# Row statistics and the splitting of rows moved to other slots, row loads and stores to SyncE, first rows prepared in another order

## The chip, the cores and the metric

The kernel runs on one core of one Trainium2 chip. The metric is the device time of one execution in microseconds. The kernel before took 2895.55 us, the median of three runs (2894.34 to 2897.94). All times below are microseconds unless they say otherwise; time points count from the start of the profiled span.

## The reference

A state-space layer makes 128 "image" rows for each of 32 sequences, 77 text rows are put behind them, and one attention block and one linear block with a residual each follow. Cut to what matters:

```python
h = concatenate([tok(log_dt, Lambda, x, 1024), txt], axis=1)   # (32, 205, 1024)
h = h + attn(layernorm(h), wq, wk, wv, wo)                     # causal, 32 heads of 32, 8 key/value heads
h = h + ffn(layernorm(h), W_base, b_base, enc0, enc1, coefs0, coefs1, mask0, mask1)
```

```python
q, k, v = x @ wq, x @ wk, x @ wv
scores = einsum('bihd,bjhd->bhij', q, repeat(k, 4)) * SCALE    # masked causally
out = softmax(scores) @ repeat(v, 4)                            # then @ wo
```

## The kernel before

The program has three stages with a barrier between them. The first (`ssm`) makes the rows `hcat` in 16 chunks of eight channels, the second (`attention`) writes the attention output `acat`, and the third (`tail`) does the output projection, the second layer norm and the linear block over 52 tiles of rows. float32 accuracy comes from products of float16 halves: a value is parted into a high half, rounded, and a low half, the rest; each product takes three matmuls (high by high, high by low, low by high).

**Steps.** `attention` is a pipeline over sequences, one a step. `steps` runs `step(b)` on each engine for b from -4 to 32; `parts(b)` says which parts a step has. In step b the scores, the softmax and the weighing of values are those of sequence b ("att"), the row maxima those of b + 1 ("max"), the q, k and v projections those of b + 2 ("qkv"), rows b + 3 are transposed ("turn") and the layer norm is that of b + 4 ("ln"). So steps -4 to -1 fill the pipeline, steps 0 to 27 are full, and steps 28 to 32 drain it. No planner orders the work: the order on each engine is the order of the code, and semaphores tie the engines together.

**Slots.** A step has eight slots g, one for each key/value head (lines 918 to 970 on VectorE, 755 to 801 on ScalarE, 1059 to 1101 on TensorE). A slot holds the q unit g and, by the table `EXTRA` (line 493), in slots 0 to 3 a second unit: v 0, v 1, k 0, k 1. A "unit" is 24 matmuls into one of two PSUM banks `psJ`; a unit waits until the unit before the last has been read out (`pj_lo`). Slot 0 also has the unit m 1 and slot 4 the unit m 0, which transpose the row maxima.

On TensorE a slot runs: two score matmuls (`scores`, L981), score rows for the maxima (`score_rows`, L1024, L1028, L1031), the first half of the q unit, the third score matmul (L984), more score rows, the second half of the q unit, `weigh` (L1010) for the slot before, the extra unit. The third score matmul takes the PSUM bank of the first and so waits for ScalarE's first exponential of the slot (`exp_done`).

On ScalarE a slot runs: three exponentials (L783), three casts into `ph` (L790, each after GpSimd's causal mask, L699), the read-out of each unit (L796, L798; each waits for its unit), and in slots 4 to 7 `high_part` (L732 and L734), which centres and scales one quarter of the rows x and casts it to `xfh`. ScalarE also issues DMAs: in slot 2 `store(b - 1, 1)` and then the copies `values` of the transposed v (L742), in slot 3 the `load` of rows b + 5, in slot 6 `store(b, 0)`. These stand ahead of the slot's exponentials.

On VectorE a slot runs: `take_maxes` (L879, L885), the low half of the last unit (`split_unit`, L893), the subtraction for `pl` (L936), then row work, then `norm` of the head before (L833, L836) and the low halves of all but the slot's last unit. The row work is `layer_norm` in slots 1 to 3 (L852 and L853 twice, then the three operations of `rsqrt_guess`) and `low_part` (L862), which writes a quarter of `xfl`: piece 0 in slot 6, pieces 1 and 2 in slot 7, piece 3 in slot 0 of the next step. GpSimd masks, does two thirds of `pl` (L704) and, after slot 3, the Newton rounds of the inverse square root (`scale_rows`, L1135 to L1138, and `nmean`, L673).

On SP (SyncE) a step issues in this order: the restacking copies of k and q halves of the step before (`restack`, L578), `m` rows (L629, L630), the transposes of rows b + 3 (`turn`, L635 high, L636 low, for the image rows and then the text rows), the restacking of k 0 and q 0 to 3, four transposes of v (L622), `m` rows again. In step 30 the weights of the tail (`ahead`, fourteen loads, L604) stand between.

**First rows.** In steps -4 and -3 the layer norm of rows 0 and 1 runs beside the splitting of the weights: ScalarE's `weights_high` (L748) and VectorE's `weights_low` (L819), eight pieces of q weights and eight of k and v weights. TensorE's first unit waits for both transposed halves of rows 0 and for the q weights, the second for the k and v weights.

**End of the first stage.** At the last chunk SP stores the peaks of the weights to memory, waits, reads them back to all partitions (L174, L176), and only then issues the four row stores of that chunk (L180).

Of the kernel before, what the change touches and what calls it, by code (L numbers as in the profile page):

```python
# [16 lines left out]
P = 128  # L17
B = 32
# [52 lines left out]
def ssm(nc, x, txt, log_dt, lam, hcat, acat, ahead, st_k, peaks, all_peaks, peaks_in):  # L71
# [5 lines left out]
    with ExitStack() as ctx:  # L77
# [82 lines left out]
        def _(sp):  # L160
# [99 lines left out]
        def _(dve):  # L260
# [112 lines left out]
            for ch in range(NCH):  # L373
# [14 lines left out]
            dve.tensor_reduce(peaks[:, 0:1], pieces[:, 0:8], AX.X, ALU.max)  # L388
            dve.tensor_reduce(peaks[:, 1:2], pieces[:, 8:12], AX.X, ALU.max).then_inc(peaks_ok, 1)
# [32 lines left out]
def attention(nc, ahead, hcat, acat, st, qkv, arena, all_peaks, peaks_in, ksc, spare):  # L422
# [7 lines left out]
    with ExitStack() as ctx:  # L430
# [36 lines left out]
        rs = sb("rs", [P, 4, 2])  # L467
        nmean = sb("nmean", [P, 2])
# [24 lines left out]
        EXTRA = {0: ("v", 0), 1: ("v", 1), 2: ("k", 0), 3: ("k", 1)}  # L493
# [79 lines left out]
        def _(sp):  # L573
# [9 lines left out]
            def step(b, par, has):  # L583
# [15 lines left out]
                if b == B - 2:  # L599

                    for q in v_in:
                        sp.wait_ge(q, 32 * B)
                    for dst, src, arrived in ahead:
                        sp.dma_start(dst, src).then_inc(arrived, 16)  # L604
                if has["turn"]:
# [3 lines left out]
                    turn(1, nxt, b + 3)  # L609
                if has["qkv"]:  # L610
# [6 lines left out]
                    wait(sp, v_ok, 2 * (b + 2))  # L617
                    if b == -2:
                        sp.wait_ge(values_ok, 1)
                    for c in range(2):  # L620
                        for k in range(2):
                            sp.dma_start_transpose(out=vt[:, k, :, c * P:(c + 1) * P], in_=vst[k][:, c, :]).then_inc(v_in[c], 16)  # L622
                if has["max"]:

                    wait(sp, pj_lo, base + at(rows, "m", 0) + 1)
                    shift_rows(0, nxt)

# [15 lines left out]
        def _(pool):  # L643
# [855 lines left out]
```

## Time and profile before

| what | us |
|---|---|
| median of three runs | 2895.55 |
| the profiled execution's own time | 2894.3 |
| its span, first to last instruction | 2891.9 |
| TensorE busy | 2655.3 (92%) |
| VectorE busy | 1941.2 (67%) |
| ScalarE busy | 1230.0 (43%) |
| GpSimd busy | 1144.9 (40%) |
| first stage | 0 to 185.3 |
| attention stage | 185.3 to 1747.0 |
| tail | 1747.0 to 2891.9 |

Busy shares are means over stages with different limits. Matmuls are pipelined, so their listed durations overlap and a busy TensorE need not be at its peak; where two stretches hold the same matmuls, the shorter one tells what was lost in the other. In a timeline a row has the start, the duration, the engine (with q: its sequencer issues a DMA), the line, the operation, output and inputs by name, the shapes and the count; in brackets stands the idle time of the engine before it and what ended it. A busy view has a stretch and its length, then for each engine its busy time and the instructions, then the granted clock of TensorE (1.00 is 2.4 GHz, 0.50 is 1.2 GHz), the busy share of the DMA engines and GB/s.

### The profile page before, as it was taken

Reading aid. Unit: us, or ns where it says so; the run is one execution under the profiler, and the core shown is the slowest. Engines: PE = TensorE matmul, PEld = TensorE weight load, DVE = VectorE, ACT = ScalarE, POOL = GpSimd, SP = SyncE. Lnnn points to the kernel's source line nnn. Section 1 sums busy time; section 2 is a strip of 40 time slices with the busy share of each in tenths; the row PEclk is TensorE's granted clock in tenths of the full one; section 3 lists DMA queues with packets and bytes.
Section 4 is the critical chain, followed back from the end, with each engine's and each line's share of the span. In section 5 each row is a group of like instructions: output and inputs, shape, how many; then the busy total and the mean of one; then the engine's idle time right before and its main releaser. Section 6 shows DMA issues by size and latency. Waiting matters only on the chain. (4 is left out here: it accounts for less than half of the span.)

```text
span 2891.9 us, 70053 instructions
## 1 busy us (share of the span) xinstructions
PE 2655.3 (92%) x27456; PEld 1919.6 (66%) x27456; DVE 1941.2 (67%) x5569; ACT 1230.0 (43%) x2570; POOL 1144.9 (40%) x1810
## 2 busy tenths in 40 slices
PE   1948999999999999999999976999999999999999
PEld 1838888888888888888888952444444444444444
DVE  8966888888888888888888674644444444444443
ACT  4343676766767676766667572201000010101010
POOL 2751565656656565666656570101010101010100
PEclk9979999999999999999999976999999999999999
DMA  7756556465555555565555454454545455545553
GB/s 242 194 122 100 98 92 105 85 109 93 96 94 96 103 93 104 84 107 92 101 92 86 73 124 170 113 139 116 133 122 136 119 134 121 133 123 131 125 129 77
DMA packets 509031, 332.99 MB, mean 115 GB/s; under 512 B 421145, under 2 KB 464409, under 8 KB 508225
## 3 DMA queue, kind: packets, MB, share of 16 engines
q1 hardware_dynamic: 486192, 264.68, 46.3%
q10 hardware_dynamic: 22512, 63.84, 7.1%
q8 instruction: 219, 3.59, 0.6%
q14 instruction: 108, 0.88, 0.1%
HBM read 116.49 MB, written 80.61 MB: 68 GB/s over the span
## 5 line engine op out<-in xcount | busy, mean ns | idle before, releaser
L1044 PE MATMUL psJ<-xth,qh 128*128 128x205 f16 x2048 | 517.3, 253 | 51.6 <-DMA xtl<-xfl 47.6
L704 POOL TENSOR_TENSOR pl<-arena,ph 128x410 f16<-128x410 f32 (+1 forms) x512 | 501.0, 998 | 94.7 <-ACT ph L790 94.7
L1046 PE MATMUL psJ<-xth,ql 128*128 128x205 f16 x2048 | 516.3, 252 | 0.0
L1045 PE MATMUL psJ<-xtl,qh 128*128 128x205 f16 x2048 | 515.8, 252 | 0.0
L699 POOL TENSOR_SCALAR_AFFINE_SELECT arena<-arena 128x256 f32<-128x256 f32 (+1 forms) x768 | 331.7, 438 | 438.3 <-ACT arena L783 419.3
L1261 POOL TENSOR_TENSOR arena<-stage,arena 128x1024 f32<-128x1024 f32 x52 | 122.1, 2349 | 936.2 <-DVE stage L1304 936.2
L1275 ACT CAST xh<-arena 128x1024 f16<-128x1024 f32 x52 | 54.3, 1045 | 995.1 <-DVE arena L1313 995.1
L783 ACT ACTIVATE arena<-psT,escale 128x410 f32<-128x410 f32 (+1 forms) x768 | 399.6, 565 | 95.5 <-PE psT L984 57.5
L790 ACT CAST ph<-arena 128x410 f16<-128x410 f32 (+1 forms) x768 | 334.8, 500 | 14.9 <-POOL arena L699 14.7
L1304 DVE SCALAR_TENSOR_TENSOR stage<-ps5O,osc,h_in 128x512 f32<-128x512 f32 x104 | 77.9, 750 | 388.4 <-PE ps5O L1401 388.4
L885 DVE TENSOR_REDUCE mx<-psS 77x2 f32<-77x410 f32 x512 | 296.5, 579 | 60.7 <-PE psS L1031 57.0
L1399 PE MATMUL ps5F<-wfh,xth 128*128 128x512 f16 x832 | 315.4, 379 | 3.4 <-DMA xtl<-xl 2.3
L1400 PE MATMUL ps5O<-wol,ath 128*128 128x512 f16 x832 | 316.1, 380 | 0.0
L1399 PE MATMUL ps5O<-woh,ath 128*128 128x512 f16 x832 | 316.1, 380 | 0.0
L1401 PE MATMUL ps5O<-woh,atl 128*128 128x512 f16 x832 | 316.0, 380 | 0.0
L1400 PE MATMUL ps5F<-wfl,xth 128*128 128x512 f16 x832 | 315.3, 379 | 0.0
L1401 PE MATMUL ps5F<-wfh,xtl 128*128 128x512 f16 x832 | 315.3, 379 | 0.0
L879 DVE CUSTOM_DVE_ANT_0 seen<-psS,mask 128x128 bf16<-128x128 f32 x1024 | 235.4, 286 | 82.7 <-PE psS L1024 82.0
L1010 PE MATMUL psO<-vh,ph 128*128 128x33 f16 (+1 forms) x3072 | 261.0, 178 | 5.0 <-issue 4.6
L1010 PE MATMUL psO<-vl,ph 128*128 128x33 f16 (+1 forms) x3072 | 260.0, 178 | 0.0
L1010 PE MATMUL psO<-vh,pl 128*128 128x33 f16 (+1 forms) x3072 | 260.0, 178 | 0.0
L1046 PE MATMUL psJ<-xth,kl 128*128 128x205 f16 x1024 | 257.8, 252 | 0.0
(231 smaller groups left out, 6106.2 us busy)
## 6 DMA issues: line engine op xcount, KB each, us to landing
a_in<-acat SPq DMA_DIRECT2D x52, 512.0 KB, 3.8
h_in<-hcat SPq DMA_DIRECT2D x52, 512.0 KB, 4.6
qst<-qsh SPq DMA_DIRECT2D x128, 205.0 KB, 4.7
out<-stage SPq DMA_DIRECT2D x51, 512.0 KB, 3.1
hcat<-ob SPq DMA_DIRECT2D x64, 256.0 KB, 4.4
xin<-hcat ACTq DMA_DIRECT2D x32, 512.0 KB
acat<-arena ACTq DMA_DIRECT2D x64, 256.0 KB
qst<-qsl SPq DMA_DIRECT2D x64, 205.0 KB, 5.7
```

The lines of the kernel that those rows point to most:

```text
L699: pool.affine_select(out=v, in_=v, compare_op=ALU.is_ge, fill=0.0, base=0, pattern=[[0, v.shape[1]], [1, w]], channel_multiplier=-1).then_ ...
L704: pool.tensor_tensor(view(pl, g % 2, k), view(p32, g % 2, k), view(ph, g % 2, k), ALU.subtract).then_inc(lo_pool, 1)
L783: act.activation(view(p32, g % 2, k), ps_view(psT[(g + k) % 2], k), ACT.Exp, scale=(escale[:, 0:1] if k < 2 else escale[0:TXT, 0:1])).then ...
L790: act.copy(view(ph, g % 2, k), view(p32, g % 2, k)).then_inc(hi_done, 1)
L885: dve.tensor_reduce(dst, v, AX.X, ALU.max).then_inc(s_read, 1)
L1010: m = pe.matmul(o[:, t, r, :], p, v[0:T[j], j, g, :], start=n == 0, stop=n == len(list_) - 1)
L1044: pe.matmul(ps[:, 0:S], wh[:, k, c], xth[:, par, k, 0:S], start=k == 0, stop=False)
L1045: pe.matmul(ps[:, 0:S], wh[:, k, c], xtl[:, par, k, 0:S], start=False, stop=False)
L1046: m = pe.matmul(ps[:, 0:S], wl[:, k, c], xth[:, par, k, 0:S], start=False, stop=k == KC - 1)
L1399: pe.matmul(ps[h][:], th[:, k, :], wh[:, k, c], start=k == 0, stop=False)
L1400: pe.matmul(ps[h][:], th[:, k, :], wl[:, k, c], start=False, stop=False)
L1401: m = pe.matmul(ps[h][:], tl[:, k, :], wh[:, k, c], start=False, stop=k == KC - 1)
```

## The change

It changes the tables of slots. Extra units move from slots 0 to 3 to slots 1 to 4. `high_part` and `low_part` now treat rows b + 3 instead of b + 4: high pieces in slots 1, 2 and 3 (two in the last), low pieces in slots 2, 3 and 4. `layer_norm` stays in slots 1 to 3 but its place is behind `low_part`, and its first piece waits for `ln_done` of the rows before; `rs` and `nmean` get two buffers. GpSimd's `scale_rows` moves to slot 4. The two copies of `values` move into slots 1 and 2, behind the casts to `ph`. `load` and `store` are issued by SP, whose order in a step is new: v transposes come ahead of the row transposes, `turn` takes the high half as soon as it is there, and the text rows' transposes come behind the restacking. The tail's small weight loads are spread over steps 1 to 13 and the 4 MB one goes to the end of step 29. In the filling steps rows 1 are loaded only once rows 0 have landed, rows 0 get their Newton rounds on VectorE, and their low halves are put between the splits of the weights. In the first stage the reductions for the peaks start two chunks earlier and their round trip starts a chunk earlier. Left out of the diff below are renamed indices (`rs[:, b % 2]`, `nmean[:, b % 2]`, `m` for `b + 4`) and GpSimd's memsets of `ph` and `pl`, which now clear only the third block.

```diff
--- before.py
+++ after.py
...
             for ch in range(NCH):
-                if ch == NCH - 1:
+                if ch == NCH - 2:
...
+                if ch == NCH - 1:
...
-                if ch >= NCH - 12:
-                    weight_peak(ch - (NCH - 12))
-            dve.wait_ge(piece_ok, 12)
...
+                if NCH - 14 <= ch < NCH - 2:
+                    weight_peak(ch - (NCH - 14))
+                if ch == NCH - 3:
+                    dve.wait_ge(piece_ok, 12)
...
         @block.tensor
...
-        EXTRA = {0: ("v", 0), 1: ("v", 1), 2: ("k", 0), 3: ("k", 1)}
+        EXTRA = {1: ("v", 0), 2: ("v", 1), 3: ("k", 0), 4: ("k", 1)}
+        HIGH, LOW, LINK = {1: (0,), 2: (1,), 3: (2, 3)}, {2: (0,), 3: (1,), 4: (2, 3)}, {1: 0, 2: 1, 3: 2}
...
-                if b == B - 2:
-                    for q in v_in:
-                        sp.wait_ge(q, 32 * B)
-                    for dst, src, arrived in ahead:
-                        sp.dma_start(dst, src).then_inc(arrived, 16)
-                if has["turn"]:
-                    wait(sp, pj_filled, base)
-                    turn(0, nxt, b + 3)
-                    turn(1, nxt, b + 3)
+                if has["last"]:
+                    store(b - 1, 1)
                 if has["qkv"]:
...
-                    wait(sp, pj_lo, base + at(rows, "k", 0) + 1)
-                    wait(sp, st_filled, 24 * b + 12)
-                    restack(K_PARTS, kst[par][:, 0:4], slice(0, 1), k_in[0])
-                    wait(sp, pj_lo, base + at(rows, "q", 3) + 1)
-                    restack(Q_PARTS, qst[par][:, 0], HALVES[0], q_in[0])
+                    wait(sp, pj_lo, base + at(rows, "v", 1) + 1)
                     wait(sp, v_ok, 2 * (b + 2))
                     if b == -2:
                         sp.wait_ge(values_ok, 1)
                     for c in range(2):
                         for k in range(2):
                             sp.dma_start_transpose(out=vt[:, k, :, c * P:(c + 1) * P], in_=vst[k][:, c, :]).then_inc(v_in[c], 16)
+                if has["turn"]:
+                    wait(sp, pj_filled, base)
+                    turn(0, nxt, b + 3)
+                if has["qkv"]:
+                    wait(sp, pj_lo, base + at(rows, "k", 0) + 1)
+                    wait(sp, st_filled, 24 * b + 12)
+                    restack(K_PARTS, kst[par][:, 0:4], slice(0, 1), k_in[0])
+                    wait(sp, pj_lo, base + at(rows, "q", 3) + 1)
+                    restack(Q_PARTS, qst[par][:, 0], HALVES[0], q_in[0])
+                if has["turn"]:
+                    turn(1, nxt, b + 3)
...
                     shift_rows(0, nxt)
+                if has["att"]:
+                    store(b, 0)
+                if has["load"]:
+                    sp.wait_ge(x_lo, 4 * (b + 4))
+                    load(b + 5, 1 - par)
+                if 1 <= b < len(ahead):
+                    dst, src, arrived = ahead[b]
+                    sp.dma_start(dst, src).then_inc(arrived, 16)
+                if b == B - 3:
+                    for q in v_in:
+                        sp.wait_ge(q, 32 * B)
+                    dst, src, arrived = ahead[0]
+                    sp.dma_start(dst, src).then_inc(arrived, 16)
+            def load(b, par):
+                sp.dma_start(xin[:, par, 0, :], hcat[b * S:b * S + P, :]).then_inc(x_in[par], 16)
+                sp.dma_start(xin[0:TXT, par, 1, :], hcat[b * S + P:b * S + S, :]).then_inc(x_in[par], 16)
+            def store(b, half):
...
+                sp.wait_ge(norm_done, 8 * b + 4 * half + 4)
+                sp.dma_start(acat[b * S:b * S + P, c], ao[:, half, 0, :]).then_inc(a_out[half], 16)
+                sp.dma_start(acat[b * S + P:b * S + S, c], ao[0:TXT, half, 1, :]).then_inc(a_out[half], 16)
...
             def turn(t, to, n):
...
+                sp.wait_ge(x_hi, 4 * n + 2 * t + 2)
+                sp.dma_start_transpose(out=xth[:, to, :, cols], in_=xfh[0:r, t, :]).then_inc(xt_in[t], 16)
...
-                sp.dma_start_transpose(out=xth[:, to, :, cols], in_=xfh[0:r, t, :]).then_inc(xt_in[t], 16)
                 sp.dma_start_transpose(out=xtl[:, to, :, cols], in_=xfl[0:r, t, :]).then_inc(xt_in[t], 16)
...
+            load(0, 0)
+            sp.wait_ge(x_in[0], 32)
+            load(1, 1)
             steps(sp, step)
...
             def scale_rows(b):
...
             def step(b, par, has):
...
-                    if has["ln"]:
+                    if has["ln"] and b > -4:
                         scale_rows(b)
...
                     if b == -3:
...
-                    if g == 3 and has["ln"]:
+                    if g == 4 and has["ln"]:
                         scale_rows(b)
...
         @block.scalar
...
-            def load(b, par):
...
-            def store(b, half):
...
-            def values(n):
...
+            def values(n, k):
...
-            load(0, 0)
-            load(1, 1)
             weights_high(0)
...
                 if b == -3:
+                    for n in range(4):
+                        high_part(0, n)
+                    n = 0
                     weights_high(1)
                 if b == -2:
...
                 for g in SLOTS:
-                    if g == 3 and has["load"]:
-                        act.wait_ge(x_lo, 4 * (b + 4))
-                        load(b + 5, 1 - par)
-                    if g == 2 and has["last"]:
-                        store(b - 1, 1)
-                    if g == 2 and has["max"]:
-                        values(b + 1)
-                    if g == 6 and has["att"]:
-                        store(b, 0)
...
                             act.wait_ge(masked, 24 * b + 3 * g + k + 1)
...
+                    if g in (1, 2) and has["max"]:
+                        values(b + 1, g - 1)
                     for kind, m in rows[g]:
...
-                    if g >= 4 and has["ln"]:
-                        high_part(b, par, g - 4)
+                    if has["turn"] and b > -3:
+                        for piece in HIGH.get(g, ()):
+                            high_part(b + 3, piece)
...
                         dve.wait_ge(x_in[par], 32 * ((b + 4) // 2 + 1))
+                        wait(dve, ln_done, b + 4)
...
+                    if b == -4:
+                        rsqrt_rounds(link, dve, rs[:, b % 2])
+                        dve.tensor_scalar(nmean[:, b % 2], mv[:, :, 0], -1.0, None, ALU.mult).then_inc(ln_done, 1)
...
-                    if has["turn"] and g == 0:
-                        low_part(b + 3, 3)
-                    if has["ln"]:
-                        if g in (1, 2, 3):
-                            layer_norm(b, par, g - 1)
-                        if b == -4 and g == 3:
-                            weights_low(0)
-                        for piece in {6: (0,), 7: (1, 2)}.get(g, ()):
-                            low_part(b + 4, piece)
-                        if b == -3 and g == 0:
-                            weights_low(1)
+                    if b == -3 and g == 0:
+                        for part, ks in (((0, 1), (4, 5)), ((2, 3), (6, 7))):
+                            for piece in part:
+                                low_part(0, piece)
+                            weights_low(0, ks)
+                        weights_low(1, range(KC))
+                    if has["turn"] and b > -3:
+                        for piece in LOW.get(g, ()):
+                            low_part(b + 3, piece)
+                    if has["ln"] and g in LINK:
+                        layer_norm(b, par, LINK[g])
+                    if b == -4 and g == NKV - 1:
+                        weights_low(0, range(4))
...
```

## Rows read from the trace of the kernel before

**Rows 1.** Busy time by stretch: stage opening, fill, 28 full steps, with granted clock (PEclk).
```profile
185.30:223.90 38.60, 0.00 (x0) 0.01 (x1) 27.38 (x50) 18.76 (x24) 23.59 (x34) 0.50 0.45 88
...
223.90:286.70 62.80, 59.42 (x658) 58.13 (x659) 36.76 (x132) 23.46 (x48) 7.99 (x39) 0.97 0.63 104
...
286.70:1588.80 1302.10, 1227.55 (x19117) 1148.37 (x19115) 1072.87 (x3665) 896.70 (x2019) 798.96 (x1483) 1.00 0.56 96
```

**Rows 2.** The same view of one step's slots 0, 1, 2, 4 and 5.
```profile
611.01:618.83 7.82, 6.72 (x105) 6.32 (x102) 6.93 (x20) 3.99 (x9) 5.32 (x7) 1.00 0.58 88
...
618.83:625.19 6.36, 6.36 (x100) 6.14 (x98) 5.65 (x19) 3.46 (x9) 3.00 (x5) 1.00 0.06 12
...
625.19:632.69 7.50, 6.55 (x100) 6.15 (x99) 5.28 (x18) 4.33 (x10) 3.00 (x5) 1.00 0.80 167
...
639.05:643.46 4.41, 4.41 (x78) 4.21 (x76) 2.92 (x13) 3.10 (x8) 3.33 (x14) 1.00 0.79 118
...
643.46:648.28 4.82, 4.61 (x76) 4.00 (x75) 3.68 (x15) 4.79 (x13) 3.35 (x6) 1.00 1.19 82
```

**Rows 3.** Waits in steps 0 to 29: us in total, times, longest.
```profile
PE psS L1028 <- DVE mx L879: 39.8, 56, 1.1
```

**Rows 4.** Timeline of ScalarE at the head of slots 3 and 5 of that step.
```profile
633.76 1.09 ACT L783 ACTIVATE arena<-psT,escale 128x410 f32<-128x410 f32 x2 [0.54 <-PE psT L981]
...
643.89 0.70 ACT L732 ACTIVATE xin<-xin,nmean 128x512 f32<-128x512 f32 x1
...
645.26 1.08 ACT L783 ACTIVATE arena<-psT,escale 128x410 f32<-128x410 f32 x2
```

**Rows 5.** Timeline of TensorE, the third score matmul of slots 3 and 5.
```profile
634.58 0.30 PE L984 MATMUL psT<-qst,kst 98*77 98x308 f16 x1
...
645.90 0.33 PE L984 MATMUL psT<-qst,kst 98*77 98x308 f16 x1 [0.18 <-ACT arena L783]
```

**Rows 6.** Timeline of SP and ScalarE at the end of the first stage.
```profile
178.10 3.24 SPq L180 DMA_DIRECT2D hcat<-ob  x4
...
176.31 0.58 ACT L246 COPY ob<-ps 128x512 f32<-128x512 f32 x1 [1.14 <-PE ps L401]
```

**Rows 7.** First rows: timelines of VectorE and GpSimd, landings of the transposes, one line group.
```profile
192.26 1.42 DVE L852 BATCH_NORM_STATS2 stats<-xin 128x6 f32<-128x512 f32 x2 [4.39 <-DMA xin<-hcat]
...
195.85 0.17 DVE L1127 TENSOR_SCALAR rs<-rs 128x2 int32<-128x2 int32 x1
...
196.26 9.66 DVE L819 SCALAR_TENSOR_TENSOR ql<-stage,qsc,qh 128x1024 f16<-128x1024 f32 x8
...
207.16 0.25 POOL L673 TENSOR_SCALAR nmean<-mv 128x2 f32<-128x2 f32 x1
...
DMA to landing us min/median/max: 3.3/6.3/9.4
...
L1127 DVE TENSOR_SCALAR rs<-rs 128x2 int32<-128x2 int32 x32 | 23.0, 720 | 1.1
```

**Rows 8.** Timeline of SP in the first fill step.
```profile
230.32 1.23 SPq L635 DMA_TRANSPOSE xth<-xfh  x1
...
247.17 5.79 SPq L622 DMA_TRANSPOSE vt<-stage  x4
```

**Rows 9.** Timelines of VectorE and GpSimd in slots 7, 7, 3 and 4.
```profile
656.82 2.12 DVE L862 SCALAR_TENSOR_TENSOR xfl<-xin,rs,xfh 128x512 f16<-128x512 f32 x2
...
656.45 3.12 POOL L704 TENSOR_TENSOR pl<-arena,ph 128x410 f16<-128x410 f32 x2 [0.38 <-ACT ph L790]
...
638.21 0.19 POOL L1135 TENSOR_TENSOR rs<-rs 128x2 f32<-128x2 f32 x1
...
641.69 1.22 POOL L699 TENSOR_SCALAR_AFFINE_SELECT arena<-arena 128x256 f32<-128x256 f32 x3
```

**Rows 10.** Timeline of TensorE in steps 30 and 31.
```profile
1687.14 0.33 PE L984 MATMUL psT<-qst,kst 98*77 98x308 f16 x1 [1.61 <-ACT arena L783]
...
1712.06 0.52 PE L981 MATMUL psT<-qst,kst 98*128 98x410 f16 x1 [4.09 <-DMA qst<-ml]
```

More of the change, by code:

```diff
@@ L384, in _ @@
                 dve.tensor_tensor(u[:, ch % 2], u[:, ch % 2], u2[:, ch % 2], ALU.add).then_inc(u_ok, 1)
-                if ch >= NCH - 12:
-                    weight_peak(ch - (NCH - 12))
-            dve.wait_ge(piece_ok, 12)
-            dve.tensor_reduce(peaks[:, 0:1], pieces[:, 0:8], AX.X, ALU.max)
-            dve.tensor_reduce(peaks[:, 1:2], pieces[:, 8:12], AX.X, ALU.max).then_inc(peaks_ok, 1)
+                if NCH - 14 <= ch < NCH - 2:
+                    weight_peak(ch - (NCH - 14))
+                if ch == NCH - 3:
+                    dve.wait_ge(piece_ok, 12)
+                    dve.tensor_reduce(peaks[:, 0:1], pieces[:, 0:8], AX.X, ALU.max)
+                    dve.tensor_reduce(peaks[:, 1:2], pieces[:, 8:12], AX.X, ALU.max).then_inc(peaks_ok, 1)
         @block.tensor
@@ L466, in attention @@
         mv = sb("mv", [P, 2, 2])
-        rs = sb("rs", [P, 4, 2])
-        nmean = sb("nmean", [P, 2])
+        rs = sb("rs", [P, 2, 4, 2])
+        nmean = sb("nmean", [P, 2, 2])
         centred, pool_ln = sem("centred"), sem("pool_ln")
@@ L598, in step @@
                     shift_rows(1, par)
-                if b == B - 2:
-                    for q in v_in:
-                        sp.wait_ge(q, 32 * B)
-                    for dst, src, arrived in ahead:
-                        sp.dma_start(dst, src).then_inc(arrived, 16)
+                if has["last"]:
+                    store(b - 1, 1)
+                if has["qkv"]:
+                    wait(sp, pj_lo, base + at(rows, "v", 1) + 1)
+                    wait(sp, v_ok, 2 * (b + 2))
+                    if b == -2:
+                        sp.wait_ge(values_ok, 1)
+                    for c in range(2):
+                        for k in range(2):
+                            sp.dma_start_transpose(out=vt[:, k, :, c * P:(c + 1) * P], in_=vst[k][:, c, :]).then_inc(v_in[c], 16)
                 if has["turn"]:
@@ L616, in step @@
                     restack(Q_PARTS, qst[par][:, 0], HALVES[0], q_in[0])
[L617 to L622, printed above, removed]
+                if has["turn"]:
+                    turn(1, nxt, b + 3)
                 if has["max"]:
@@ L671, in scale_rows @@
                 pool.wait_ge(dve_ln, 9 * (b + 5))
-                rsqrt_rounds(links, pool, rs)
-                pool.tensor_scalar(nmean[:], mv[:, :, 0], -1.0, None, ALU.mult).then_inc(ln_done, 1)
+                rsqrt_rounds(links, pool, rs[:, b % 2])
+                pool.tensor_scalar(nmean[:, b % 2], mv[:, :, 0], -1.0, None, ALU.mult).then_inc(ln_done, 1)
             links = Chain(pool, pool_ln)
@@ L739, in values @@
                 wait(act, av_done, 8 * (n - 1))
-                for k, dst in enumerate((vh, vl)):
-                    v = vt[:, k].rearrange("p t (g d) -> p t g d", d=HD)
-                    act.copy(dst[n % 2][:, :, :, 0:HD], v).then_inc(v_ok, 1)
+                v = vt[:, k].rearrange("p t (g d) -> p t g d", d=HD)
+                act.copy((vh, vl)[k][n % 2][:, :, :, 0:HD], v).then_inc(v_ok, 1)
             def weights_high(n):
@@ L814, in _, with weights_low @@
             dve.wait_ge(cleared, 1)
-            def weights_low(n):
-                for k in range(KC):
+            def weights_low(n, ks):
+                for k in ks:
                     dve.wait_ge(w_hi, n * KC + k + 1)
@@ L861, in low_part @@
                 dve.wait_ge(x_hi, 4 * m + n + 1)
-                dve.scalar_tensor_tensor(xfl[0:r, t, c], xin[0:r, m % 2, t, c], rs[0:r, 3, t:t + 1], xfh[0:r, t, c],
+                dve.scalar_tensor_tensor(xfl[0:r, t, c], xin[0:r, m % 2, t, c], rs[0:r, m % 2, 3, t:t + 1], xfh[0:r, t, c],
                                          ALU.mult, ALU.subtract).then_inc(x_lo, 1)
```

27 lines of the change are left out of this document (11 added, 16 removed).

## The prediction

> **What bounds the kernel now.** I began with the stretches of the execution [rows 1]. The reader is to see three things: in the 28 full attention steps TensorE is busy 1227.6 of 1302.1 us at full clock, 46.50 us a step; nothing runs on it in the 38.6 us that open the stage; and the two fill steps after them take 62.8 us. The tail stays as it is. Then I read one step slot by slot [rows 2]. A slot with a q unit, an extra unit and nothing late takes 6.36, one with a q unit and a max transposition 4.41, with TensorE busy all through. Less some 0.17 for that transposition, a bare slot is 4.24 and a unit 2.12 (estimates). TensorE alone would need 6.53 + 3 x 6.36 + 4.41 + 3 x 4.24 = 42.74 a step. The other 3.76 are stalls: 1.29 in slot 0, some 0.9 to 1.1 in slot 2, 0.58 in slot 5, the rest in 6 and 7.
>
> Who makes them? In slots 7 and 0 the score-row matmuls wait for VectorE, 39.8 us over steps 0 to 29 [rows 3]: its xfl pieces hold it back there. In slots 2 and 5 it is ScalarE. The third score matmul of a slot needs the slot's first exponential. Slot 3 begins at 632.69, its exponential comes 1.07 in and the matmul 1.89 in, unhindered. Slot 5 begins at 643.46; one high piece of x stands ahead of the exponential, which comes 1.80 in, and the matmul 2.44 in, 0.55 late [rows 4, 5]. A piece costs ScalarE 645.26 - 643.89 = 1.37. The matmul follows a late exponential by 0.64, so the exponential may come up to 1.25 in at no cost.
>
> **The change, part by part.**
> (a) *End of the first stage.* The last four row stores go out at 178.10, behind the round trip of the peaks, though the copy they need ends at 176.89 [rows 6]. With the round trip a chunk earlier: -1.2. The peak reductions move two chunks up on VectorE, into chunks as long as those they leave; I put that at nothing. Without that cover it is a reduction or two, at most +2.5.
>
> (b) *First rows.* Today the statistics begin at 192.26; GpSimd's rounds end with nmean at 207.4, slowed beside VectorE's eight splits of q weights (9.66), and only then are the rows parted; TensorE starts at 223.9 [rows 1, 7]. After, from the stage's new start at 184.1: one step's rows are loaded alone. They land 6.9 after the first issue today, with twice the bytes under way; I take 5, between that and half. Statistics and guess take 4.0 (192.26 to 196.26), twelve small operations and nmean on VectorE 2.6 at 0.2 apart (a guess operation took 0.17 here, 0.72 on average in the full steps [rows 7], so 2.2 to 9), four weight splits 4.8, two xfl pieces 1.4, two splits 2.4, two pieces 1.4: 205.7 to 206. The last transpose lands 3.3 after its issue where no row load is beside it and up to 9.4 where one is [rows 7]. The load now stands behind it on SP; I take 3.6. TensorE starts at 209.7, 25.6 after the stage's start instead of 38.6: -13.0, give or take 4.
>
> By the Trainium skill, *DMA: Bandwidth & Descriptors*, Issuing engines are not separate DMA queues, DMAs interleave on the same 16 engines whoever issues them. By that rule the load still slows the last transpose, and the start would be nearer 215.5. The trace agrees for a load issued beside the transposes; none shows one issued behind them.
>
> (c) *Fill.* Rows n+3 are now parted in the step before TensorE needs them. In the first fill step: q unit 0 at the half clock that the idle stretch leaves [rows 1] takes 4.1 (twice 2.1), then units of 2.1; VectorE stands in slot 1 at its new wait for ln_done of the rows before, with the splits of two units queued behind it, so TensorE waits some 2.0 and 3.5. The second v unit is split at 228.4. From there SP issues four v transposes (5.8), two x transposes (1.3 each), six copies at about 0.6, two more x transposes [rows 8]: 242.9, landed near 246, where TensorE is ready at 242.7. The next step (29.5 of TensorE's work) ends near 275.5 and waits for ml, which SP issues behind the same row, until 277.5. The fill takes 67.8 instead of 62.8: +5.0, bounds 0 and +10.
>
> (d) *Full steps.* Slot 0 loses its extra unit and its piece, slots 5 to 7 their pieces, slot 2 the two stores and the value copies ahead of its exponential (the copies now stand behind the casts to ph, beside TensorE's unit). But in slots 1 to 3 each high piece stands behind the cast of the extra unit, which ends with the slot: it is still ahead of the next exponential. So slots 2 and 3 each get slot 5's 0.58. Slot 3 has two pieces: slot 4's exponential comes 1.80 + 1.37 = 3.17 in, the third score matmul 3.83 in, 1.94 late. VectorE then has pl at about 5.2, two xfl pieces from 5.7 (2.12 for two beside GpSimd [rows 9]), the norm (0.58) and the q split, to 8.7. The max transposition stands behind two units there and needs that split; TensorE is there at 8.3: 0.4 more. Slot 4: 6.53 + 1.94 + 0.38 = 8.85. GpSimd's subtractions (3.12 beside such pieces) end at 8.8, its 13 small operations take 3.48 more (638.21 to 641.69 [rows 9]), so slot 5's first mask comes 3.4 in; today it comes 2.64 into slot 4 and costs nothing there. Slot 6's exponential then comes 1.14 in, just inside 1.25, and VectorE's reads 0.17 late. Sum: 4.41 + 6.36 + 6.94 + 6.94 + 8.85 + 4.24 + 4.41 + 4.24 = 46.39; with 0.06 for disturbed steps 46.45 against 46.50: 28 x -0.05 = -1.4. The part that moves most should bring next to nothing. Bounds per step: 42.9 (no stall left) and 48.5 (VectorE or GpSimd 2 us behind).
>
> Row loads and stores on SP: six issues of some 0.35 to 0.6 a step, and one of 13 small weight loads in steps 1 to 13. SP reaches the last x transpose of a step some 37 us in; it lands by 41 to 46.4 and is needed at 47.2. I cost this at nothing; the cover is 1 to 6 us.
>
> (e) *End.* Step 28 now parts rows in slots 1 to 3 (+1.1), step 29 parts none and ScalarE stores nothing (-1.2). In step 30 the wait of 1.61 behind stores and values goes, and in step 31 the 4.09 for qst<-ml, which stood behind fourteen weight loads on SP [rows 10]: they are spread now, the 4 MB one a step earlier. -5.7; up to 3 come back if that one delays the restacking copies.
>
> Against the profiled execution's own 2894.3: -1.2 - 13.0 + 5.0 - 1.4 - 0.1 - 5.7 = -16.4, so 2877.9. The median of the runs is 1.25 above that execution: 2879.
>
> **Rivals.**
> *GpSimd's rounds become the bound (slower).* Place: slots 4 to 6. The two late xfl pieces stretch GpSimd's subtractions, the rounds follow at once, then slot 5's masks. Slot 6 has 0.1 us to spare; beyond it each microsecond is one a step. If they end 1 us later than worked out: 28 x 0.9 = +25, 2904. For it: VectorE's small operations took 0.2 to 0.7, GpSimd's pair up to 3.12. Against: today's rounds cost TensorE nothing. 0.16.
> *The steps lose what start and end give.* In slots 2 and 3 VectorE's q split comes 1.3 into the next slot, 0.5 after TensorE wants it; I hid that behind the late score matmul. If 0.4 a step show: +11, 2890. 0.14.
> *The last transpose shares with the load:* start 5.8 later, 2885. 0.10.
> *Pieces hide better:* without the 0.38, the 0.17 and one 0.58, 28 x -1.1: 2848. 0.11. All hidden, 42.9 a step: 28 x -3.6, 2779; the order in the code speaks against it. 0.04.
>
> **Numbers.** The forecast, steps of 46.1 to 46.8, has 0.45, its own range is 2867 to 2891. A measurement of this kernel tells some 0.2%, 5.8 us, from no change. Faster by more: 0.45 + 0.10 + 0.11 + 0.04 = 0.70; within: 0.14; slower by more: 0.16. The range reaches from the better case short of 2779 to the slower one: 2850 to 2904.
>
> **What would show it.** First TensorE matmul of the stage near 210; the first scores of step 0 near 277 instead of 286.8; slot 4 near 8.9, with a wait of psT L984's line for ScalarE near 1.9; no waits behind the mx reads in slots 7 and 0; none for qst<-ml at the end. I am wrong if a step is under 45.5 or over 47.2, if TensorE's first unit waits for weights and not for x, or if slot 0 of a step waits for a DMA.

## The result, and the profile after

The change made the kernel slower by 0.4%: 2909.06 us median of 5 runs (2905.7 to 2913.93) against 2897.4 before (five runs; the table ahead of the prediction has the first three), ratio 1.004 with a 95% interval of 1.0024 to 1.0055. Forecast were 2879 us and a range that ended at 2904. The profiled execution took 2905.7 us, its span is 2904.0, 12.1 longer than that of [rows 1].

First the stretches of the changed kernel: from the end of the first stage to TensorE's first unit, the fill, the 28 full steps (the view of [rows 1], columns as there).

```profile
184.60:210.56 25.96, 0.00 (x0) 0.03 (x1) 22.10 (x47) 18.77 (x24) 10.13 (x18) 0.50 0.40 102
210.56:286.01 75.45, 63.56 (x658) 60.18 (x659) 44.69 (x148) 19.78 (x43) 9.09 (x42) 0.92 0.51 85
286.01:1608.54 1322.53, 1229.35 (x19116) 1148.40 (x19117) 1074.03 (x3663) 898.28 (x2017) 783.39 (x1483) 1.00 0.51 96
```

TensorE starts 13.4 us sooner, but the fill takes 75.45 instead of 62.84, so that step 0 begins at 286.01, where it began at 286.76. The 28 steps take 1322.5 instead of 1302.1 us: 47.23 each. Steps 28 to 31, counted to the first scores of the last slot, take 139.6 instead of 147.2. In sum -0.75 + 20.4 - 7.6 = +12.05, the whole difference: what comes behind takes 1155.8 in one and 1155.9 in the other.

Step 8 of the changed kernel, slots 0 to 5, as in [rows 2]; slots 6 and 7 take 4.24 each as well:

```profile
663.92:668.47 4.55, 4.55 (x81) 4.20 (x78) 3.41 (x14) 3.04 (x7) 3.29 (x6) 1.00 0.62 109
668.47:675.03 6.56, 6.53 (x100) 6.14 (x98) 6.10 (x21) 3.76 (x9) 3.82 (x7) 1.00 0.48 88
675.03:681.97 6.94, 6.54 (x100) 6.15 (x98) 5.42 (x15) 5.04 (x11) 3.46 (x5) 1.00 0.06 18
681.97:688.95 6.98, 6.53 (x99) 6.13 (x98) 6.54 (x22) 4.56 (x10) 3.46 (x5) 1.00 0.10 21
688.95:698.36 9.41, 7.00 (x101) 6.20 (x100) 7.26 (x21) 6.19 (x13) 4.76 (x10) 1.00 0.64 123
698.36:702.61 4.25, 4.25 (x76) 4.08 (x75) 2.90 (x13) 3.31 (x8) 3.25 (x13) 1.00 1.21 135
```

TensorE's waits from 200 to 1700 us (us in total, times, longest), the answer to [rows 3]:

```profile
PE psT L1009 <- ACT arena L797: 59.7, 59, 1.8
...
PE psJ L1077 <- DVE qsl L916: 22.1, 29, 0.8
PE psJ L1069 <- DVE qsl L916: 17.7, 30, 3.1
PE psS L1049 <- DMA qst<-qsl: 3.7, 1, 3.7
PE psT L1006 <- DMA qst<-ml: 2.4, 1, 2.4
```

The waits behind the mx reads are gone from the steps, as forecast. In their place stands the third score matmul's wait for ScalarE (slots 2 and 4 of 28 steps), and a wait for VectorE's split of the q unit, ahead of slot 4's max transposition (22.1) and of slot 3's unit (12.7 of the 17.7; the rest are two waits in the fill, 1.83 and 3.13). The two engines in slot 4, where [rows 4] had the one piece of slot 5:

```profile
689.15 0.33 ACT L814 CAST ksh<-psJ 128x205 f16<-128x205 f32 x1 [2.39 <-PE psJ L1071]
689.38 0.72 ACT L755 ACTIVATE xin<-xin,nmean 77x512 f32<-77x512 f32 x1
...
691.50 0.72 ACT L757 ACTIVATE xfh<-xin,rs 77x512 f16<-77x512 f32 x1
692.13 1.51 ACT L797 ACTIVATE arena<-psT,escale 128x410 f32<-128x410 f32 x3
```
```profile
694.10 0.59 DVE L959 TENSOR_TENSOR pl<-arena,ph 128x410 f16<-128x410 f32 x1
694.60 2.67 DVE L885 SCALAR_TENSOR_TENSOR xfl<-xin,rs,xfh 77x512 f16<-77x512 f32 x2
...
697.76 0.36 DVE L916 TENSOR_TENSOR qsl<-psJ,qsh 128x205 f16<-128x205 f32 x1
```

ScalarE sits idle for 2.39 us until the extra unit is done, reads it out, and only then makes two high pieces; the slot's first exponential comes 3.18 in (forecast 3.17). VectorE's q split stands behind two xfl pieces, which take 2.67 together.

### The profile page after: what moved, and what is told of

It is laid out like the page before. It is cut to its first block and busy times, and to the rows that moved or that the text cites. A ratio compares the mean times of both kernels' runs of the same rounds, so it can differ in the third digit from the quotient of the medians.

```text
span 2904.0 us, 70147 instructions
## 1 busy us (share of the span) xinstructions
PE 2655.0 (91%) x27456; PEld 1918.0 (66%) x27456; DVE 1946.6 (67%) x5582; ACT 1231.9 (42%) x2570; POOL 1114.4 (38%) x1797
## 5 line engine op out<-in xcount | busy, mean ns | idle before, releaser
L737 POOL TENSOR_TENSOR pl<-arena,ph 128x410 f16<-128x410 f32 (+1 forms) x512 | 474.0, 946 | 94.6 <-ACT ph L804 94.6
L1069 PE MATMUL psJ<-xth,kh 128*128 128x205 f16 x1024 | 257.8, 252 | 1.8 <-DVE qsl L916 1.8
```

Source lines behind the costliest of these rows:

```text
L737: pool.tensor_tensor(view(pl, g % 2, k), view(p32, g % 2, k), view(ph, g % 2, k), ALU.subtract).then_inc(lo_pool, 1)
L1069: pe.matmul(ps[:, 0:S], wh[:, k, c], xth[:, par, k, 0:S], start=k == 0, stop=False)
```

## The experiments

Two theories of the steps. **A**: ScalarE's high pieces stand in the wrong place, behind the extra unit and ahead of the exponential. **V**: VectorE has too much to do in slots 1 to 4. Of the fill: **B**: the later parting gave the 13 us back; its rival, a limit that both layouts share. Every figure of the table is from the kernel's profiled execution: TensorE's first unit, first scores of step 0, the 28 full steps and one of them on average, steps 28 to 31 (to the last slot's first scores), and the median of the runs beside its ratio to the kernel before with the interval.

```
kernel             unit    step 0   28 steps  one    28-31  median   ratio (interval)
before             223.92  286.76   1302.1   46.50   147.2  2897.4
after              210.56  286.01   1322.5   47.23   139.6  2909.06  1.0040 (1.0024-1.0055)
after_again        209.44  285.65   1321.9   47.21   146.4  2907.47  1.0034 (1.0022-1.0047)
e1_pieces_first    209.46  287.32   1254.4   44.80   141.0  2841.35  0.9808 (0.9794-0.9822)
e2_two_mv          210.30  282.89   1320.7   47.17   139.6  2902.09  1.0018 (1.0008-1.0028)
e3_first_rows      214.03  285.57   1303.9   46.57   147.6  2893.42  0.9987 (0.9979-0.9996)
e4_sync_ends       216.94  288.28   1271.9   45.42   143.4  2862.68  0.9882 (0.9869-0.9896)
e5_low_last        209.22  287.02   1207.6   43.13   142.3  2797.45  0.9653 (0.9637-0.9669)
e6_extra_later     218.14  290.29   1289.4   46.05   142.3  2880.48  0.9944 (0.9932-0.9956)
e7_fill_order      209.31  280.36   1320.9   47.18   139.6  2901.86  1.0022 (1.0012-1.0032)
e8_one_a_slot      208.46  283.76   1287.6   45.98   142.4  2873.59  0.9919 (0.9906-0.9932)
e9_all             209.35  281.84   1205.9   43.07   135.6  2786.73  0.9615 (0.9601-0.9628)
e10_scalar_issues  213.22  291.54   1338.5   47.80   143.4  2934.44  1.0135 (1.0119-1.0150)
```

**e1: the high pieces ahead of the extra unit's read-out.**

```diff
-                    for kind, m in rows[g]:
+                    for which, (kind, m) in enumerate(rows[g]):
+                        if which == 1 and has["turn"] and b > -3:
+                            for piece in HIGH.get(g, ()):
+                                high_part(b + 3, piece)
```

> The changed kernel with one thing moved: in slots 1 to 3 ScalarE's high pieces of x come between the read-out of the q unit and that of the extra unit (where ScalarE sat idle for 1.87, 1.86 and 2.39 us of slots 1, 2 and 3 in the trace of after), not behind the latter. Theory A (the steps are long because the pieces stand ahead of the next slot's exponential): the waits of 0.40 in slot 2 and 1.65 in slot 4 go, the step falls from 47.2 to about 45.2, 28 x 2.0 = 56 us, the time to some 2853; ScalarE's read-out of slot 3's extra unit comes 0.5 late, which costs nothing. Theory V (VectorE is the bound in slots 2 to 4: its two statistics, two xfl pieces and norm end behind TensorE there anyway, as in the waits of 0.45 and 0.76 for its q split): TensorE comes sooner and waits for q splits instead, the step stays above 46.3, the time above 2884.

A holds, and with more than its price: the step falls by 2.43 to 44.80, the time to 2841. Slot 4 of step 9 takes 7.58; ScalarE at its head (it begins at 715.38):

```profile
713.09 0.72 ACT L755 ACTIVATE xin<-xin,nmean 77x512 f32<-77x512 f32 x1
...
715.22 0.72 ACT L757 ACTIVATE xfh<-xin,rs 77x512 f16<-77x512 f32 x1
715.85 0.31 ACT L817 CAST ksh<-psJ 128x205 f16<-128x205 f32 x1
716.06 1.09 ACT L797 ACTIVATE arena<-psT,escale 128x410 f32<-128x410 f32 x2
```

The pieces now fill the idle time before the unit, and the exponential comes 0.68 in. Slot by slot: slot 2 falls by 0.59 to 6.35, slot 4 by 1.83 to 7.58, and slot 3 not at all (6.98), although a high piece no longer stands ahead of its exponential. V is right in one point: the waits for q splits stay to the tenth (22.1 and 12.8), the only ones of any size left in the steps, and slot 3's is the one that held it.

**e5: e1, and the low pieces behind norm and q split on VectorE.** `low_part` moves from behind pl to behind the slot's first `split_unit`.

> The kernel with the high pieces ahead of the extra unit's read-out (e1_pieces_first: 2841 us, step 44.74 with slots 4.56 6.56 6.35 6.98 7.58 4.24 4.23 4.24), and in it the low pieces moved on VectorE from behind pl to behind the norm and the q split of the slot. Theory Q (what is left is the q split that stands behind the xfl pieces, which run at 1.5 instead of 0.75 us beside GpSimd's subtraction): the waits of 0.45 in slot 3 and 0.76 in slot 4 go, slot 3 falls to 6.4, slot 4 to 6.7, the step to 43.3, the time by 28 x 1.4 = 40 to about 2801. Rival (VectorE simply has too much to do in slots 2 to 4, whatever its order): the maxes of the next slot come late instead, the step stays above 44.4 and the time above 2830.

Both waits go. Slots 3 and 4 take 6.36 and 6.53 (0.62 and 1.05 less than in e1), the step 43.07 in nearly all of them; 2797.45 us. Each xfl piece also halves. The tile xfl on VectorE (min/median/max ns of one) in the kernel before, then in the changed one:

```profile
L862 DVE SCALAR_TENSOR_TENSOR xfl<-xin,rs,xfh x79: 739/1448/1498, 605.7 to 1496.3; 128x512 f16<-128x512 f32 x40, 77x512 f16<-77x512 f32 x39
L885 DVE SCALAR_TENSOR_TENSOR xfl<-xin,rs,xfh x78: 1250/1494/1500, 600.3 to 1499.2; 77x512 f16<-77x512 f32 x40, 128x512 f16<-128x512 f32 x38
```

and in e5, where GpSimd's pl subtraction is over, or within 0.1 us of it, when the piece starts (half of the pieces find GpSimd idle, half find it at 128x2 operations):

```profile
L888 DVE SCALAR_TENSOR_TENSOR xfl<-xin,rs,xfh x84: 735/742/777, 606.9 to 1481.4; 128x512 f16<-128x512 f32 x42, 77x512 f16<-77x512 f32 x42
```

So VectorE had time enough; the piece was long because GpSimd's pl subtractions ran beside it. Where one of the two must wait, it need not be VectorE: in the kernel before, the first piece of slot 7 takes 744 ns beside a subtraction (656.82), and that subtraction takes 1932 ns where 964 is the median. GpSimd's pl in the kernel before:

```profile
L704 POOL TENSOR_TENSOR pl<-arena,ph x311: 763/964/1942, 601.2 to 1499.9; 128x410 f16<-128x410 f32 x156
```

By the Trainium skill, *SBUF — State Buffer*, Who interferes with whom, a VectorE operation with two SBUF inputs and a GpSimd operation that reads SBUF exclude each other for a whole instruction. The trace agrees: 1494 against 742 ns for the same piece.

**e8: the changed kernel with one piece a slot.** `HIGH = {1: (0,), 2: (1,), 3: (2,), 4: (3,)}`, `LOW = {2: (0,), 3: (1,), 4: (2,), 5: (3,)}`.

> The changed kernel with one number changed: one high piece in each of slots 1 to 4 and one low piece in each of slots 2 to 5, all still behind the extra unit's read-out. Theory A's price list (a high piece ahead of an exponential 0.5 to 0.6, a second one 1.37 more) gives slot 4 9.41 - 1.37 - 0.4 = 7.6 or less, and puts 0.58 into slot 5 and, since slot 5 has no room on VectorE for a low piece of 1.5, up to 0.7 into slot 6: step 46.3 +- 0.4, 28 x 0.9 = 25 less, time about 2884. If only the place behind the extra unit matters and not the number (rival), the step stays at 47.2.

Slot 4 falls to 7.12, slot 5 rises to 4.86 (+0.62), slot 6 to 4.73 (+0.49): 45.98, at the lower end of what A gave: the number of pieces ahead of one exponential matters. The gain is half of e1's, since a piece still stands ahead of an exponential: the third score matmul waits in slots 2, 4 and 5 of every step (0.40, 0.28 and 0.43). The run spreads the low pieces as well, so it does not part the price of the second high piece from that of the pair of low ones: the wait for the q split in slot 4 goes too.

**e4: the kernel before with stores, loads and `ahead` as in the change.**

> The kernel before with only this changed: row loads and stores issued by SyncE instead of ScalarE, and the loads for the tail spread over the steps instead of all in step 30. Theory D (drain gain is the spreading): steps 28 to 31 lose the wait of 4.09 for qst<-ml and part of 1.61: 147.2 to about 141. In the full steps slot 2 loses the two issues ahead of its exponential (some 0.4 to 0.7 of its 1.0 stall): 28 x 0.5 = 14 us. Together -20, 2877. Rival 1 (issues are cheap and the value copies alone make slot 2's stall): steps stay at 46.4 to 46.5 and the time is 2891. Rival 2 (SP's queue delays a transpose that TensorE needs): a wait of TensorE for a DMA appears in slot 0, steps above 46.6, time at 2897 or above.

The part that had no price of its own in the forecast is worth most: 1.08 a step. Slot 2 takes 6.62 instead of 7.33 on average, slot 6 4.23 instead of 4.61, slot 3 6.36 instead of 6.41; the single steps of 47.0 to 47.6 us that the kernel before has are gone. The drain gives 3.8, less than expected. TensorE also starts 7 us sooner (216.94): the third rows' load now stands behind the four transposes on SP, and TensorE starts 3.1 behind the last one's issue (213.85), where it was 8.7 before. The fill takes that back: a wait for a q split of 8.72 stands in it.

**e6: e4, and the value and key units in slots 1 to 4.** `EXTRA = {1: ("v", 0), 2: ("v", 1), 3: ("k", 0), 4: ("k", 1)}`.

> The kernel e4_sync_ends (old parting, row loads and stores on SyncE, 2862.7 us, step 45.36) with one thing more of the change: the value and key units in slots 1 to 4 instead of 0 to 3. It tells what the place of the units does without the place of the parting. If the units' place is harmless: slot 0 gives 2.12 and some of its 1.3 of stall, slot 4 grows to 6.53, the high piece in slot 4 then stands behind the extra unit's read-out and puts 0.6 into slot 5: step 44.9 to 45.4, time 2850 to 2864. If the units' place costs by itself (slot 4 holds the max transposition too), the step is above 45.9 and the time above 2877, and the parting's place is to be charged with less than the 1.8 us a step between this kernel's base and the changed one.

46.05: put on top of e4, the units' place costs 0.63. Its waits, 290 to 1625 us:

```profile
PE psS L1030 <- DVE mx L881: 39.8, 56, 1.1
PE psJ L1046 <- DVE qsl L895: 14.2, 29, 1.0
PE psT L986 <- ACT arena L785: 13.7, 29, 1.6
```

The mx waits stay (they belong to the xfl pieces in slots 6, 7 and 0, not to the units), and a q split and an exponential come late in addition. So in this order the change adds up, a step, from: issues -1.08, units' place +0.63, and all the rest, the parting's place above all, 47.23 - 46.05 = +1.18; in sum +0.73. The rest also holds the value copies, the place of GpSimd's rounds and SP's order, which no run parts from it.

**e10: the changed kernel with stores and loads back on ScalarE.** Stores ahead of the exponentials of slots 2 and 6, the load ahead of slot 6's.

> The changed kernel with the row stores and loads given back to ScalarE (stores ahead of the exponentials of slots 2 and 6 as in the kernel before, the loads ahead of slot 6's). Moving them took 46.50 - 45.42 = 1.1 us a step off the kernel before. If that holds in the changed order too, the step grows from 47.2 to 48.0 to 48.5 (slot 2 by 0.7 to 1.1, where a high piece already makes the exponential late, slot 6 by 0.4 to 0.9), and the time to 2909 + 28 x 1.0 = 2937. Rival (the issues hide behind the new order's longer slots): step 47.2 to 47.4, time 2909 to 2915.

The time is as expected (+27 against the changed kernel run again), the way is not: the steps grow by 0.59 (slot 2 by 0.26 to 7.20, slot 6 by 0.33), 16.5 in all, and step 0 begins 5.9 later, behind a wait of 5.81 for ml. In the changed order a good part of ScalarE's issues is hidden: 0.59 instead of 1.08. The two figures are not of quite the same thing, since the loads stand in slot 6 here and stood in slot 3 before.

**e3: the kernel before with the first rows alone sooner.** The rounds of step -4 on VectorE, one load first, `weights_low(0, ...)` in parts between the xfl pieces; all later rows in the old place.

> The kernel before with only the first rows changed (one step's rows loaded first, by SyncE; their rounds and nmean on VectorE; four weight splits, two xfl pieces, two splits, two pieces, and so on; each transpose issued as soon as its operand is there). All later rows are parted in the old place, four steps ahead. Theory B (the 13 us won at the start were given back because the parting of the next rows was moved a step later, into the fill): TensorE starts 13 us sooner and the fill stays near 63: 2897.4 - 12.5 = 2885. Rival (the fill is limited by something both layouts share, the order on SP or VectorE's own work): the fill grows to 70 or more and the time is within 6 us of 2897.

B falls. With the old parting, too, 8.7 of the 9.9 us that the start gains are lost again: the fill takes 71.5, step 0 begins 1.2 sooner, and the time is 4 us less. TensorE's longest wait there, and ScalarE ahead of it:

```profile
229.81 0.35 PE L1059 MATMUL psJ<-xth,qh 128*128 128x205 f16 x1 [9.63 <-DVE qsl L902]
```
```profile
223.12 0.72 ACT L740 ACTIVATE xin<-xin,nmean 128x512 f32<-128x512 f32 x1 [14.52 <-POOL nmean L681]
...
228.59 0.31 ACT L804 CAST qsh<-psJ 128x205 f16<-128x205 f32 x1
```

The second rows are parted in program order ahead of the read-out of the first rows' units. What brings the first rows forward runs into the second ones, here and in e4 (8.72), and these depend on VectorE (k weight splits, statistics) and GpSimd. In the kernel before, with its late start, the wait at this place is 2.96. In the changed kernel, which parts these rows later, the waits here are 1.83 and 3.13, but others come behind them, and step 0 begins no sooner than in e3.

**e2 and e7: what holds the changed fill.** e2 doubles mv and lets the statistics wait for `ln_done` of the rows two steps back. e7 is e2 with SP's order changed in the fill.

```diff
-                        wait(dve, ln_done, b + 4)
+                        wait(dve, ln_done, b + 3)
```

> The changed kernel with mv doubled, so that the statistics wait for the scaling of the rows two steps back and no longer for ln_done of the rows just before. Theory F1 (the new wait is what lengthens the fill): VectorE's wait of 3.35 us in the fill goes, and with it the stalls of TensorE of 1.83 and 3.13 and the half clock behind them (some 1.7): the fill falls from 75.4 to about 69 and the time by 6, to 2903. Theory F2 (SP's order is what sets the end of the fill: v transposes, x transposes, then the restacking): what is won before 240 is waited for again at the scores' first use of the restacked q (3.70 in after) and at ml (2.44): the fill stays at 74 to 75 and the time within 2 us of 2909. Full steps as in after, 47.2.

> The kernel e2_two_mv (2902 us; step 0 begins at 282.9, with waits of 3.39 for the restacked q at the first score rows and of 2.20 for ml) with SyncE's order changed in the two fill steps alone: in the first the restacking of K and Q goes ahead of both x transposes, in the second the rows of m ahead of the last x transpose. Theory F2 (what is left of the fill's growth is SP's order): the 3.39 falls to 1 to 2.5, which is then a wait for x, the 2.20 to under 1, step 0 begins at 280 +- 1, the time falls by 2 to 4 to about 2899. Rival (the x transposes are as late as the restacking was): both waits keep their sum within 1 us, under the new name of xth, and nothing is won.

e2: the 3.13 goes and step 0 begins 3.1 sooner, half of what F1 gave. The 1.83 stays (1.99), and so does the half clock: TensorE is busy 12.5 us of the fill at a granted clock of 0.50, against 11.3 in the changed kernel. The wait at the first score rows is still 3.39:

```profile
245.94 0.29 PE L1049 MATMUL psS<-kst,qst 96*128 96x128 f16 x1 [3.39 <-DMA qst<-qsl]
...
282.89 0.35 PE L1006 MATMUL psT<-qst,kst 98*128 98x410 f16 x1 [2.20 <-DMA qst<-ml]
```

e7: that wait is 0.25, but the next unit is late instead. The view names no releaser ("issue"); that it is x, now transposed later, is argued from the order and not shown. The wait for ml stays:

```profile
241.34 0.40 PE L1054 MATMUL psS<-kst,qst 96*128 96x128 f16 x4 [0.25 <-DMA qst<-qsl]
...
244.97 0.33 PE L1074 MATMUL psJ<-xth,qh 128*128 128x205 f16 x1 [2.99 <-issue]
...
280.36 0.52 PE L1011 MATMUL psT<-qst,kst 98*128 98x410 f16 x2 [2.32 <-DMA qst<-ml]
```

Step 0 begins at 280.4, as F2 had it, but not by F2's mechanism: the waits shown sum to 5.6 in both kernels, which is the rival's mark. What differs is that TensorE starts 1.0 sooner and is busy only 7.6 us of the fill at the half clock instead of 12.5; a wait of 1.99 stands in both fills, the clock falls behind it in e2 and not in e7. The median doesn't move either (2901.86 after 2902.09), so no gain of e7's order is shown.

In e7's profile the tail takes 1159.8 us, in e2's 1155.5; the other kernels' tails lie near one or the other. The difference goes with the granted clock again. The stretch of the tail from 34 us behind the last slot's first scores to the output projection's first matmul, in e2 and in e7:

```profile
1777.19:1811.62 34.43, 32.96 (x49) 11.20 (x49) 25.16 (x29) 0.00 (x0) 0.00 (x0) 0.65 0.30 87
```
```profile
1774.84:1813.02 38.18, 36.33 (x48) 12.32 (x49) 26.70 (x31) 0.00 (x0) 0.00 (x0) 0.59 0.29 79
```

**e9: e5, mv doubled, and e7's order.**

> The three edits together: high pieces ahead of the extra unit's read-out, low pieces behind the q split (both as in e5_low_last, 2797.5 us, step 0 at 287.0), mv doubled, and SyncE's order of e7_fill_order in the fill. If the fill's waits and the steps' waits are independent: step 0 begins at 280.5, steps 43.07, 2797.5 - 6.5 = 2791. Rival: the high pieces, which come ahead of the extra units' read-outs in the fill too, stand there in the way of the fill's units (step 0 began 1 us later in both kernels that have them), and the fill keeps 3 of the 6.5: 2794.

2786.73 us, 3.85% under the kernel before and 4.2% under the changed one: the gains add up within 5 us, with luck in it: step 30 ran at the full clock here (25.69 us), so steps 28 to 31 take 135.6 instead of e5's 142.3. Step 0 begins at 281.84, 1.5 later than in e7. That the high pieces cost the fill this is not shown: TensorE is busy 9.9 us of this fill at the half clock and 7.6 of e7's, which is 1.2 of the 1.5.

**The changed kernel run again.**

> The changed kernel itself, to compare on the same chip as the others: 2909 +- 4 us, ratio to the kernel before 1.004.

The same time, but another profile at the end. Step 30 of this execution, then of the first one:

```profile
1698.69:1730.54 31.85, 28.31 (x402) 21.85 (x400) 25.45 (x107) 24.10 (x52) 26.34 (x40) 0.53 0.37 106
```
```profile
1698.73:1724.39 25.66, 20.09 (x403) 15.62 (x400) 24.45 (x107) 22.99 (x51) 23.16 (x40) 1.00 0.50 146
```

The same instructions from the same moment take 31.85 us at a granted clock of 0.53 and 25.66 at 1.00. Step 30 has no units, and the clock may fall in it or not.

## Why the prediction was wrong, step by step

(a) *End of the first stage*, -1.2: the row load is issued at 184.91, some 0.4 to 0.7 sooner. Too large, and of no account.

(b) *First rows*, start at 209.7: 210.56, near what was worked out (the last low piece came 1.6 late, since the small operations took 3.5 us and not 2.6 and the stage began 0.5 later; the last landing was 0.7 quicker). SP issued the last transpose at 207.64 and the row load right behind it:

```profile
207.64 1.20 SPq L666 DMA_TRANSPOSE xtl<-xfl  x1
208.89 0.58 SPq L648 DMA_DIRECT2D xin<-hcat  x1
```

TensorE starts 2.9 after the transpose's issue, and 3.1 in e4; with a load beside it, it took up to 9.4 [rows 7]. The rival that they share fell, and with it what the Trainium skill's *DMA: Bandwidth & Descriptors* (Issuing engines are not separate DMA queues), read as in the prediction, would have made of the start: 215.5.

(c) *Fill*, +5.0: **failed**, +12.6. The four waits were in the sum and came near: 2.0, 3.5, 3.3 and 2.0 forecast, 1.83, 3.13, 3.70 and 2.44 measured. Missed were two things. The second fill step's work was put at 29.5; the kernel before takes 32.2 for it (254.57 to 286.76). And the clock comes down again inside the fill; I had counted the half clock for the first unit alone (4.1). The stretches of the changed kernel's fill at 1.2 GHz, then the only one of before's and what stands behind its wait of 2.96:

```profile
210.56:215.71 5.15, 4.63 (x27) 3.74 (x28) 5.15 (x9) 0.33 (x1) 0.00 (x0) 0.50 0.40 146
225.96:229.36 3.40, 3.40 (x22) 2.99 (x21) 1.81 (x4) 0.33 (x1) 0.00 (x0) 0.50 0.02 5
249.86:253.26 3.40, 3.30 (x21) 2.74 (x22) 1.43 (x9) 0.00 (x0) 0.00 (x0) 0.50 1.11 294
```
```profile
223.92:228.27 4.35, 4.35 (x26) 3.83 (x27) 0.03 (x1) 1.57 (x3) 2.92 (x13) 0.50 0.00 0
...
233.36:240.00 6.64, 6.64 (x76) 6.64 (x77) 3.85 (x9) 0.73 (x3) 0.00 (x0) 1.00 0.71 78
```

The second stretch stands behind the wait of 3.13, the third behind that of 3.70. TensorE is busy 11.3 us at the half clock; against the 4.1 counted, half of the difference is lost: 3.6. With the 2.7 of work, 0.5 for a wait for kl and 0.3 by which the four waits were longer in sum, 67.8 becomes 74.9 of 75.4. The forecast thus gave back 5.0 of the start's 13 where the fill took 12.6.

(d) *Full steps*, -1.4: **failed**, +20.4. Slots 2, 3 and 5 to 7 came within 0.18 of the forecast; slot 4 took 9.41 instead of 8.85, slot 1 6.56 instead of 6.36, slot 0 4.56 instead of 4.41. 28 x (0.56 + 0.20 + 0.15 + 0.04 - 0.18) = 21.6, and 21.8 was missed.

Two mechanisms were in the forecast, and e1 and e5 price them apart. High pieces ahead of an exponential (the changed kernel less e1): 0.59 in slot 2, nothing in slot 3, 1.83 in slot 4, 2.42 in all; forecast were 0.58, 0.58 and 1.94, 3.10. VectorE's q split behind the xfl pieces (e1 less e5): 0.62 in slot 3 and 1.05 in slot 4, 1.67 in all; forecast were nothing and 0.38. So the right sum for slot 3 is luck: its 0.58 was booked to the high piece, and it was the q split that showed, with the late exponential hidden behind it, and not the other way round. The mechanisms were right; the mis-sized term is the q split, 0.38 a step where it took 1.67 (0.76 in slot 4 by the listed wait alone), and 0.2 more in slot 1, where TensorE's weight load waits 0.24 for it in all of these kernels, e5 too. I had taken 2.12 for the two xfl pieces of slot 4 from [rows 9]; there one of the two went unhindered at GpSimd's cost (see e5), and here the pair took 2.67. In sum -0.68 + 1.29 + 0.20, and +0.17 in slot 0, which no run explains, and -0.18 in slot 6, make 0.80, where 0.78 lie between 46.45 and 47.23. That is the second rival, with 1.3 to 1.5 a step more than the forecast held where it had 0.4, and it decided the sign. The forecast's bigger error lies beneath the sum: I let terms of 1 to 3 us a step cancel, and took the 0.05 that was left as the result.

(e) *End*, -5.8: -7.6. The waits of 1.61 and 4.09 are gone, as forecast, but that the number is near is luck: step 30's clock was 0.71 on average before and 1.00 in this execution. In the second one, at 0.53, the end gives only 0.8. The two executions differ by 6.5 us, most of the 8.2 between the kernel's fastest and slowest run.

The slower rival named GpSimd: its time (2904) was near, its mechanism absent. The rounds end 2.3 into slot 5, and slots 5 to 7 take 4.24 each. That pieces hide better fell too. Of the three marks of an error one came, and barely: a step over 47.2. Step 0's first scores, near 277 by the forecast, came at 286.01.

## What to carry to other kernels

Before moving work into a gap, look where in the in-order stream the gap opens: the same four pieces of 1.4 us were free in the steps ahead of the instruction that ScalarE waited at, and cost 2.4 a step behind it. Where small terms of both signs cancel, each has to be priced from the rows beside which it will run (a VectorE piece next to GpSimd's subtractions took twice its time), and the sum's range is that of the terms. A start that comes sooner is worth what the next rows allow: follow them to the first full step before it is booked.

## What the runs showed of the hardware

- The same xfl piece on VectorE: 742 ns in the median with no subtraction of GpSimd's beside it (e5), 1494 beside one (the changed kernel). In the kernel before it could go the other way: a piece of 744 ns beside a subtraction of 1932.
- Taking six DMA issues a step off ScalarE gave 1.08 us a step, and the odd long steps (slots 3 and 6 of the kernel before, up to 7.0 and 5.5) went with them.
- A DMA transpose with a row load issued 1.25 us behind it on the same queue landed in at most 2.9 us; with loads issued by ScalarE beside them, transposes took up to 9.4 [rows 7].
- TensorE's granted clock fell to 0.50 behind waits of 3.13 and 3.70 us in the changed kernel, but not behind one of 2.96 before; behind a wait of 1.99 at the same place it fell in e2 and stayed in e7. In step 30 of one and the same kernel it was 0.53 in one execution and 1.00 in another: 6.2 us apart.
